# Decoder layer with routed experts: SyncE holds the last scatter waits, and residual rows come as two transfers of four batches

## The reference

```python
x = _layernorm(x + _L0_attn_ref(x, ...))          # one head; softmax(QK^T/16) V, then W4 and b4
x = _layernorm(x + _L0_xattn_ref(x, ctx, mask, ...))  # cross attention (375 keys, 16 heads), self attention, GELU feed-forward
x = _layernorm(x + _L0_ffn_ref(x, ...))           # each token to one of 8 experts, mixed with a sigmoid weight
```

## Time and profile before

| What | us |
|---|---|
| three timed runs, median | 436.35 |
| three timed runs, lowest and highest | 435.93, 436.43 |
| the profiled execution, its own time | 435.29 |
| its span in the profile | 433.5 |
| PE busy | 406.1 |
| DVE busy | 274.8 |
| ACT busy | 244.4 |
| POOL busy | 126.0 |

### The profile page before, as it was taken

The page is one execution under the profiler, slowest core; times in us unless marked ns, Lnnn a source line. Parts: engine busy times, 40 slices in busy tenths (PEclk is TensorE's granted clock), DMA queues, the critical chain, the costliest instruction groups (busy, mean ns, idle before and its releaser), DMA issues.

```text
span 433.5 us, 10642 instructions
## 1 busy us (share of the span) xinstructions
PE 406.1 (94%) x3736; PEld 343.3 (79%) x3736; DVE 274.8 (63%) x949; ACT 244.4 (56%) x824; POOL 126.0 (29%) x257
## 2 busy tenths in 40 slices
PE   7969999999999999999999999999999798999990
PEld 7736787878878778787887888877888697899990
DVE  5566676777677777677786716669778644444531
ACT  0202786599777888898889986766122023333330
POOL 5161104223113231131310403325446303642221
PEclk9989999999999999999999999999999789999996
DMA  7942152510000105100000007910780411321000
GB/s 217 279 104 101 38 175 52 182 66 9 10 26 29 38 2 211 38 17 4 1 2 2 4 2 299 432 46 1 272 344 22 154 38 28 99 66 34 26 26 14
DMA packets 11031, 38.02 MB, mean 88 GB/s; under 512 B 1520, under 2 KB 6352, under 8 KB 9328
## 3 DMA queue, kind: packets, MB, share of 16 engines
q1 hardware_dynamic: 9184, 32.05, 21.7%
q0 software_dynamic: 1248, 3.18, 2.2%
q10 hardware_dynamic: 544, 2.08, 1.6%
HBM read 32.27 MB, written 5.04 MB: 86 GB/s over the span
## 4 chain that ended last, share of the span: by engine, by line
PE 60%; DVE 7%; ACT 7%; issue 2%; POOL 1%; DVEq 0%; ACTq 0%; POOLq 0%
PE bank_scores L791 9%; PE bank_pt L680 8%; PE bank_out L816 8%; PE bank_out L702 5%; PE bank_out L725 5%; PE bank_pt L715 5%; PE bank_out L557 4%; PE bank_out L543 4%; PE bank_scores L664 3%; PE bank_out L550 3%; ACT arena L1230 2%; ACT arena L1219 2%; DVE arena L1001 1%; PE bank_scores L670 1%; ACT arena L1239 1%
## 5 line engine op out<-in xcount | busy, mean ns | idle before, releaser
L1219 ACT ACTIVATE arena<-arena,negmaxc 112x375 f32<-112x375 f32 x128 | 76.6, 604 | 17.1 <-DVE negmaxc L1001 16.7
L1239 ACT ACTIVATE arena<-bank_pt 125x448 f32<-125x448 f32 (+1 forms) x128 | 66.6, 547 | 34.8 <-PE bank_pt L680 34.7
L1001 DVE CUSTOM_DVE_ANT_0 arena<-bank_scores,arena 112x375 f32<-112x375 f32 x128 | 65.2, 543 | 18.4 <-PE bank_scores L670 12.4
L680 PE MATMUL bank_pt<-ident,arena 112*125 112x112 f32 (+1 forms) x512 | 74.7, 276 | 1.8 <-ACT arena L1239 1.2
L680 PEld LDWEIGHTS bank_pt<-ident,arena 112*125 112x125 f32 (+1 forms) x512 | 63.1, 175 | 15.1 <-ACT arena L1239 5.8
L557 PE MATMUL bank_out<-arena 128*112 128x256 f32 (+1 forms) x224 | 56.5, 383 | 0.1
L1272 ACT ACTIVATE arena<-bank_scores,consts 128x128 f32<-128x128 f32 x80 | 22.9, 368 | 57.5 <-PE bank_scores L791 57.5
L1317 POOL TENSOR_TENSOR vareps<-meanvar,scal 112x1 f32<-112x1 f32 (+1 forms) x50 | 9.7, 194 | 126.0 <-DVE meanvar L880 90.6
L1230 ACT ACTIVATE arena<-bank_scores,negmaxs 112x112 f32<-112x112 f32 x128 | 43.4, 354 | 3.4 <-DVE negmaxs L1007 2.8
L557 PEld LDWEIGHTS bank_out<-arena 128*112 128x112 f32 (+1 forms) x224 | 37.7, 181 | 7.8 <-DVE arena L931 0.5
L791 PE MATMUL bank_scores<-arena 128*128 128x128 f32 x320 | 39.7, 285 | 2.5 <-issue 1.8
(11 more groups left out here) (170 smaller groups left out, 649.2 us busy)
## 6 DMA issues: line engine op xcount, KB each, us to landing
arena<-moe SPq DMA_DIRECT2D x8, 2048.0 KB, 12.5
arena<-ctxT SPq DMA_DIRECT2D x8, 375.0 KB, 3.1
arena<-mask SPq DMA_DIRECT2D x8, 164.1 KB, 3.5
arena<-x_slots SPq DMA_DIRECT2D x9, 130.0 KB, 2.1
x_slots<-arena SPq DMA_DIRECT2D x8, 130.0 KB, 2.7
arena<-weights SPq DMA_DIRECT2D x1, 1024.0 KB, 5.3
arena<-fi SPq DMA_DIRECT2D x1, 1024.0 KB, 6.4
arena<-fo SPq DMA_DIRECT2D x1, 1024.0 KB, 8.3
```

The source lines that it names most:

```text
L680: last = nc.tensor.transpose(dst[0:kp, j * S:(j + 1) * S], probs[0:S, (n % 2) * HG + j, c * kp:(c + 1) * kp], ident[0:S, 0:S])
L1001: v.tensor_tensor_reduce(out=probsC[0:S, i % (2 * HG)], in0=score_bank[j][0:S, 0:KX], in1=masks[0:S, u % 2], scale=-1.0, scalar=3.0e38, op ...
L1219: a.activation(probsC[0:S, i % (2 * HG)], probsC[0:S, i % (2 * HG)], ACT.Exp, bias=negmax["c"][0:S, u, at:at + 1], scale=-1.0, accum_out=s ...
L1239: a.activation(probsT[0:kp, n % RT, c], pt_bank[PT[stage, i] % RP][0:kp, 0:HG * S], ACT.Copy).then_inc(pt_free, 1)
```

## The change

The first edit splits the residual rows otherwise: L468 brings batches 0 to 3, L480 batches 4 to 7, and POOL's additions for batches 2 and 3 wait for the first transfer. The second edit takes the waits for the scatters of tiles 6 and 7 off the end of POOL's stream and puts them at the end of SP's.

```diff
-            sp.dma_start(resid[0:S, 0:2], xrow[:, 0:2]).then_inc(xrow_first_in, 16)
+            sp.dma_start(resid[0:S, 0:4], xrow[:, 0:4]).then_inc(xrow_first_in, 16)
...
-                    sp.dma_start(resid[0:S, 2:8], xrow[:, 2:8]).then_inc(xrow_in, 16)
+                    sp.dma_start(resid[0:S, 4:8], xrow[:, 4:8]).then_inc(xrow_in, 16)
...
+            for j in (E - 2, E - 1):
+                sp.wait_ge(y_sent[j % 2], 16 * (j // 2 + 1))
...
-                    pool.wait_ge(xrow_first_in if i < 2 else xrow_in, 16)
+                    pool.wait_ge(xrow_first_in if i < 4 else xrow_in, 16)
...
-            for j in (E - 2, E - 1):
-                pool.wait_ge(y_sent[j % 2], 16 * (j // 2 + 1))
```

## The result

| | before, same chip | changed | ratio, 95% interval |
|---|---|---|---|
| median, us | 436.14 (435.05 to 436.43, 4 runs) | 430.47 (430.19 to 431.36, 4 runs) | 0.9868 (0.9842 to 0.9893) |
| profiled execution | 435.29, span 433.5 | 430.6, span 428.9 | |

The change gains 5.67 us where 3.8 were forecast. Between the two profiled executions the gain is 4.7 us. One and the same kernel takes a few microseconds more or less from one execution to the next, because its early loads land at other times; that turns out to be the main point of this case. A ratio leaves out executions more than 1.5% above the fastest of their kernel, which concerns three of the twelve of e13_delay_busy alone.

What follows compares the result with a forecast made beforehand. TensorE, busy 94% of a 433.5 us span, was taken as the bound. Stall 2.55 plus clock 1.17 (3.7) and final waits 0.1 made 3.8 us, so the median 436.35 became 432.6, range 431.2 to 434.8.

Steps and rivals of the forecast that it cites:

- Edit 1, the landing: Start of the run: the larger first residual transfer lands at 14.7 us, bounds 14.7 to 21.7, before POOL's first addition.
- Edit 1, the stall: PE's gap before batch 3's L618 shrinks from 2.59 to about 0.4 us; first keys product L550 starts 2.55 earlier.
- The clock: Around the first keys product, PE's clock no longer falls near 30 us: 1.17 us gained.
- Carried through: From the second keys product to the end of the run, the 3.7 us gained at the start is kept whole.
- the fourth rival: Gain lost again further on, by the expert stage's head or work timed by early DMAs: 435.6 to 436.2 us; chance 0.11.
- Edit 2: End of POOL's stream: moving two final waits to SP gains 0.1 us, bounds 0 and 0.3; the drain stays.
- The sum: Whole kernel: 3.7 + 0.1 = 3.8 us gained, giving 431.5 for the profiled execution and 432.6 for the median.
- The range's lower end: Whole kernel: 431.2 us, for a median as good as the profiled execution or a shorter late low-clock stretch.
- The clock falls all the same: Second keys product and after: three short PE gaps still lower the clock, costing 1.7 us; 434.3 in all; chance 0.22.
- The larger transfer late: Start: first residual transfer lands at 21.7 us, delaying POOL and DVE; 0.4 us slower, 436.8 in all; chance 0.03.
- SP's wait frees POOL: End of the run: last scatter and POOL's drain overlap, giving up to 2.2 us more, 430.4; chance 0.04.
- Given back later: PE is stopped again further on, at the expert stage's head or by early DMAs: 435.6 to 436.2 us; chance 0.11.

Runs made afterwards that it cites:

- e13_delay_busy: Changed kernel plus 11 dependent powers on POOL ahead of the third addition and eight identity matmuls on PE ahead of batch 3's L618: 437.62 us, ratio 0.9959.
- e3_before_again: The kernel before, no line changed, built again as a kernel of its own: 437.34 us against 436.42, ratio 0.9975.
- second pair: Profiles of the kernel before and the changed kernel, each built again without a changed line; the second keys product stands 6.24 us earlier in the latter.
- e15_pool_free_again: Changed kernel with POOL waiting for no scatter and SP waiting for all used tiles, second run: 430.21 us, ratio 0.9849.

## Why the prediction was right in its place and wrong in its size

**Edit 1, the landing.** Taken 14.7, measured 15.6, inside the bounds and with 0.5 us to spare before POOL's 16.17. The additions as one group and ScalarE's copy as what is late next: both as written. The transfers put behind it lost more than the "about 1 us" and landed later than written (the late `xT` at 25.0 instead of 22.2, the second `xrow` at 28.2 instead of 25.0), but no wait for them shows.

**Edit 1, the stall.** "2.55 earlier" for the first keys product: between the two first profiles it is 3.10, less 0.70 that lies ahead of the change, 2.40. For the execution that was read, the term is right. It doesn't hold for every execution of the kernel: in e3_before_again it is 31.02 - 26.11 = 4.91, less 0.52, 4.4.

**The clock.** "1.17 gained": 3.67 - 2.59 = 1.08 between keys products in the first pair, 3.92 - 2.59 = 1.33 in the second. Ahead of the first keys product, L618 to L550 takes 2.04 in the long stall, 1.87 in the mild one and 1.60 in the changed kernel. In the mild one the clock is still at its upper level there, so at most the 0.17 between the first two can be the clock's.

**Carried through.** Right at the last matmul: 4.18 at the second keys product, 4.33 there. In the second pair 1.3 us were given back, 0.9 of it within the late low stretch of different length between L747 and L791. That is the mechanism of the fourth rival, in the kernel before.

**Edit 2.** "I take 0.1", bounds 0 and 0.3; the rows show 0.22.

**The sum, and the step that failed.** 431.5 was forecast for the profiled execution; it took 430.6, of which 0.7 is a better start. That start varies without the change: L618 of batch 2 stands at 23.67 to 24.20 in four profiles with the old loads, at 23.32 to 23.93 in four with the new ones. The failed step is the last one: "the median of the three timed runs is 436.35, 1.06 above, and gives 436.35 - 3.8". It took a gain that was read from one execution for the gain of the median, and so the 1.06 us for time that the change leaves alone. In the changed kernel nothing of it is left: its profiled execution took 430.6, its median is 430.47. The terms that were too small for the median are the stall and the clock behind it. The landing of the second `xrow` transfer varies (25.0, 24.8, 26.5, 26.4 in four profiles), and where it is late the two terms are 4.4 and 1.3 us instead of the 2.55 and 1.17 of the sum. With 0.2 for edit 2 that makes 5.9, beside measured gains of 5.67, 6.5 and 5.8; the short stall makes 3.7. That the median behaves like the long stall is therefore inferred from these gains and from the mean clocks, not seen in each timed execution. The range's lower end, "a median as good as the profiled execution", took the 1.06 into account but no longer stall. "About 0.2%" for what the measurement can tell was too small as well: the kernel against itself gave 0.25%.

**The rivals.** *The clock falls all the same*: refuted; 1.00 in every stretch until 336 us, behind gaps of 0.46, 0.75 and 0.60. The Trainium skill (TensorE: Matmul & The Clock Gate, A second HAM failure mode: psum-queue depth-cycling) has the clock swing when PE pauses shortly and often between groups; at this place the trace doesn't bear that out. *The larger transfer late*: refuted, 15.6 where it was to decide from 21.3 on. *SP's wait frees POOL*: not in this change, but right as a further edit, with 1.4 us instead of 2.2. The Trainium skill's figure (VectorE: DVE Perf Modes, The DRAIN you can't avoid) of some 12 ns for such drains on all engines holds here for SP with 7 ns, and not for POOL with 2201 to 4752 ns. *Given back later*: not between the two first profiles.

## What to carry to other kernels

A stall that ends with a DMA's landing should be priced from several executions, because the landing moves and the one profile may be the mildest; what lies between a profiled execution and the median may be the very stall that the edit removes. Here that is the likely reading, not a proven one. After a long gap, add what the clock does behind it, and ask in which executions it does so. If one engine's drain is long, let another engine hold the last waits: all of them, since a single one left behind keeps the drain in the path.

## What the runs showed of the hardware

- POOL's drain at the end took 2201 ns in every profile where it began after the scatters had landed, and 4377 to 4752 ns where it began before, ending 1.12 us after the landing. SP's took 7 ns, PE's 8 (72 and 73 in the two kernels with extra matmuls), DVE's 96 or 97, ACT's 183 to 189.
- Early loads land at different times from execution to execution: the constants, issued by SP, between 5.0 and 6.9 us; the second `xrow` of the kernel before and of the two whose loads are the same, between 24.8 and 26.5; `xT` of batches 2 and 3 between 8.5 and 10.9 in thirteen of the seventeen profiles, at 11.8 in one, and at 12.5, 13.0 and 13.3 in three.
- Gaps of PE of 2.43, 2.57, 2.59 and 2.86 us each had 3.4 us at 1.2 GHz behind them. Gaps of 3.39, 4.38, 4.41 and 4.58 each came with 6.8 us at 1.2 GHz, and there the clock fell before PE began again. The gap of 1.27 us at 11.9 us (e15_pool_free_again) and those of 1.75 us near 361 to 372 us had no low clock behind them.
- The same kernel built and loaded twice differed by 0.25% on one chip, with an interval that leaves out 1.
